# A token tower with a two-expert feed-forward: weight rows stored in pieces, and a first stage with its order and its products rewritten

## What is computed

```python
# token stage (the part that the change touches most)
def vgcn(word_emb, gv_ids, adj, W, b):
    ev = word_emb[gv_ids]                         # 128 table rows for each sequence
    H = jnp.einsum('bgh,bhd->bgd', adj, ev)
    return relu(H.mean(axis=1) @ W.T + b)         # 16 features for each sequence
emb = word_emb[input_ids] + pos_emb
graph = concat([vgcn(...adj0), vgcn(...adj1), vgcn(...adj2)])   # repeated over the 128 tokens
y = layernorm(concat([emb, graph]) @ W_proj.T + b_proj)
# second stage: y + long convolution of layernorm(y) along the batch-major sequence of tokens
h = y + fft_conv(layernorm(y), k) + bias * layernorm(y)
# third stage: 8 experts, 2 for each token
logits = layernorm(h) @ Wr.T;  top-2, softmax over the two
out = h + sum_k w_k * (gelu(x @ Wi[e_k].T + bi[e_k]) @ Wo[e_k].T + bo[e_k])
```

## Time and profile before

| what | us |
|---|---|
| median of 3 runs | 1231.76 |
| the profiled execution's own time | 1239.12 |
| its span in the profile | 1237.3 |
| TensorE busy | 878.2 |
| VectorE busy | 639.1 |
| ScalarE busy | 540.3 |
| GpSimd busy | 674.0 |

### The profile page before, as it was taken

How to read it: one execution, slowest core, us unless ns; L and a number is a source line. 1 busy time by engine, 2 the same in 40 slices (tenths; PEclk the granted TensorE clock), 3 DMA queues, 4 the chain that set the end, 5 groups by cost and what they waited for, 6 DMA issues and landing times. The chain is left out here.

```text
span 1237.3 us, 22985 instructions
## 1 busy us (share of the span) xinstructions
PE 878.2 (71%) x7442; PEld 775.1 (63%) x7442; DVE 639.1 (52%) x2223; ACT 540.3 (44%) x1323; POOL 674.0 (54%) x608
## 2 busy tenths in 40 slices
PE   1544444654444547495875799998988998999991
PEld 0433333443333435495874689998988998998991
DVE  2043434453534354537868745664655565655661
ACT  1021212121212123354855757665655766676760
POOL 6455554655554650002530057776866887878874
PEclk9966666666666667696556989998999999999996
DMA  6234343543535351591088054477477446434442
GB/s 202 74 106 143 108 143 116 147 156 96 163 87 168 95 178 36 144 285 55 1 233 270 3 169 80 59 169 178 57 176 213 62 94 162 62 56 62 62 52 30
DMA packets 119542, 146.94 MB, mean 119 GB/s; under 512 B 13476, under 2 KB 105799, under 8 KB 117415
## 3 DMA queue, kind: packets, MB, share of 16 engines
q0 software_dynamic: 39552, 53.26, 23.1%
q1 hardware_dynamic: 78902, 82.31, 21.8%
q10 hardware_dynamic: 1008, 10.34, 2.1%
HBM read 107.05 MB, written 38.82 MB: 118 GB/s over the span
## 5 line engine op out<-in xcount | busy, mean ns | idle before, releaser
L880 ACT ACTIVATE Hs<-bank,U 128x256 bf16<-128x256 f32 x426 | 211.9, 497 | 183.7 <-PE bank L708 154.0
L517 POOL DMA_INDIRECT out<-Hs,si x142 | 236.9, 1669 | 85.5 <-issue 85.2
L1202 DVE TENSOR_TENSOR Hs<-Hs 128x512 bf16<-128x512 f32 x213 | 147.5, 692 | 148.2 <-ACT Hs L881 134.5
L575 PE MATMUL bank<-ev_g,diag 128*12 128x192 f32 x384 | 96.1, 429 | 179.8 <-ACT diag L759 172.1
L478 POOL DMA_INDIRECT ev_g<-in_word_emb,idx x192 | 185.0, 964 | 58.5 <-issue 58.5
L508 POOL DMA_INDIRECT blob<-xtab_d,gi x142 | 149.0, 1049 | 123.5 <-DVE gi L1187 84.2
L881 ACT ACTIVATE Hs<-bank,U 128x256 f32<-128x256 f32 x426 | 214.0, 502 | 0.0
L723 PE MATMUL bank<-U,Hs 128*128 128x192 bf16 x852 | 213.0, 250 | 0.2 <-issue 0.2
L725 PE MATMUL bank<-U,Hs 128*128 128x192 bf16 x852 | 211.4, 248 | 0.0
L724 PE MATMUL bank<-U,Hs 128*128 128x192 bf16 x852 | 211.1, 248 | 0.0
L575 PEld LDWEIGHTS bank<-ev_g,diag 128*12 128x12 f32 x384 | 44.0, 118 | 231.7 <-issue 119.5
(11 more groups left out here) (184 smaller groups left out, 1726.5 us busy)
## 6 DMA issues: line engine op xcount, KB each, us to landing
U<-blob_d SPq DMA_DIRECT2D x20, 771.0 KB
U<-blob_d SPq DMA_DIRECT2D x20, 672.0 KB
adj_s<-in_adj SPq DMA_DIRECT2D x48, 256.0 KB
ev_g<-kpad_d SPq DMA_DIRECT2D x24, 512.0 KB, 6.2
wst<-in_wsrc SPq DMA_DIRECT2D x8, 1344.0 KB
blob_d<-blob ACTq DMA_DIRECT2D x7, 1443.0 KB
xtab_d<-U SPq DMA_DIRECT2D x4, 1552.0 KB, 8.9
out<-Hs SPq DMA_DIRECT2D x4, 1536.0 KB, 10.9
```

The lines of the kernel that those rows point to most:

```text
L517: pool.indirect_dma_start(out, bass.IndirectOffsetOnAxis(ap=si[:, q % RX, h:h + 1], axis=0), yo[:, q % RX, h, :], None, compute_op=ALU.add ...
L575: last = mm(bank[3][0:KG, 0:D], diag[:, p, k, :], ev_g[:, p, j, b, :], start=k == 0, stop=k == KG - 1)
L880: f(hh[w][:, d, :], ps, ACT.Gelu, bias=bi[:, d:d + 1])
L1202: last = v.tensor_tensor(hl[w][:, c:c + 2, :], hf[w][:, c:c + 2, :], hh[w][:, c:c + 2, :], ALU.subtract)
```

## The change

Two things are in the diff. The prepared weights go to DRAM as `up_d` and `down_d`, each in 6 pieces, so that a run for one partition is 1028 or 896 bytes. And the first stage is rewritten: the index copy goes, and gathers take their indices straight from `ids_i`, in an unrolled loop; the embedding gathers wait on `emb_t` of the quad two before, and only those for `ev_g` on `gvec`; `adj_s` is loaded with four consecutive rows of a matrix in one partition (2048 bytes in one run) and the column means add up over four products with a block-wise `mean_w`; TensorE does the column means of quad i + 1 ahead of the graph vectors of quad i; the graph vectors are computed transposed, with `ev_g` as the weights and one column of means as the moving side, so that `diag`, `grow_s` and the transposes of the result go; `wg` is padded with zeros to 128 columns.

```diff
-        blob_d = nc.dram_tensor("blob_d", (E, 128, BLOB), fp32).ap()
+        up_d = nc.dram_tensor("up_d", (E, PIECES, 128, UP // PIECES), fp32).ap()
+        down_d = nc.dram_tensor("down_d", (E, PIECES, 128, DOWN // PIECES), fp32).ap()
+
+        def pieces(room):
+            return room.rearrange("p (n x) -> p n x", n=PIECES)
+
+        def of_expert(pieces_d, e):
+            return pieces_d[bass.ds(e, 1), :, :, :].rearrange("e n p x -> p (e n) x")
...
         def store_expert(eng, e):
             eng.wait_ge(w_lo, e + 1)
-            eng.dma_start(blob_d[bass.ds(e, 1), :, :].rearrange("e p x -> p (e x)"), blob[:, :]).then_inc(w_out, 16)
+            eng.dma_start(of_expert(up_d, e), pieces(blob[:, 0:UP])).then_inc(w_out, 16)
+            eng.dma_start(of_expert(down_d, e), pieces(blob[:, UP:BLOB])).then_inc(w_out, 16)
...
             def load_adj(i, p):
                 for j in range(GRAPHS):
-                    sp.dma_start(adj_s[:, p, j, :, :],
-                                 t["adj"][j][bass.ds(i * Q, Q), :, :].rearrange("b g h -> g b h")).then_inc(adj_in[p], 16)
+                    sp.dma_start(adj_s[:, p, j, :, :].rearrange("p r h -> p (r h)"),
+                                 t["adj"][j][bass.ds(i * Q, Q), :, :].rearrange("b (c r) h -> (b c) (r h)", r=Q)).then_inc(adj_in[p], 16)
...
             def load_up(e, w):
-                sp.dma_start(wbuf[w][:, 0:UP], blob_d[bass.ds(e, 1), :, 0:UP].rearrange("e p x -> p (e x)")).then_inc(wi_in[w], 16)
+                sp.dma_start(pieces(wbuf[w][:, 0:UP]), of_expert(up_d, e)).then_inc(wi_in[w], 16)
...
-            def gathers(i, p):
-
-                if not (isinstance(i, int) and i < 2):
-                    pool.wait_ge(gvec, i - 1)
-                nc.gpsimd.tensor_copy(idx[:, p, :].rearrange("p (j b) -> p j b", b=Q), ids_i[:, :, bass.ds(i * Q, Q)]).then_inc(idx_staged, 1)
-                pool.wait_ge(idx_staged, i + 1)
-                pool.sem_inc(pool_turn, 1)
+            def gathers(i):
+                p = i % 2
+                after(pool, emb_t, i - 1)
                 for b in range(Q):
                     pool.indirect_dma_start(emb_g[:, p, b, :], None, t["word_emb"],
-                                            bass.IndirectOffsetOnAxis(ap=idx[:, p, b:b + 1], axis=0)).then_inc(emb_in[p], 16)
+                                            bass.IndirectOffsetOnAxis(ap=ids_i[:, 0, i * Q + b:i * Q + b + 1], axis=0)).then_inc(emb_in[p], 16)
+                after(pool, gvec, i - 1)
                 for j in range(GRAPHS):
...
-            def quad(it, p):
-                i = 2 * it + p
-                pe.wait_ge(adj_in[p], 16 * GRAPHS * (it + 1))
+            def column_means(n, i, p):
+                pe.wait_ge(adj_in[p], 16 * GRAPHS * n)
+                after(pe, cs_ready, i)
...
+            def graph_vectors(it, i, p):
+                pe.wait_ge(cs_ready, i + 1)
+                after(pe, gfeat_ready, i)
                 pe.wait_ge(ev_in[p], 16 * KG * (it + 1))
...
+                        mm(bank[3][:, k:k + 1], ev_g[:, p, j, b, 0:D0], cs[:, p, k:k + 1], start=True, stop=True)
+                        last = mm(bank[3][:, 16 + k:17 + k], ev_g[:, p, j, b, D - 128:D], cs[:, p, k:k + 1], start=True, stop=True)
...
+                    i = 2 * it + p
+                    turn_embeddings(it, i, p)
+                    if not (isinstance(i, int) and i == NQ - 1):
+                        column_means(it + 1 + p, i + 1, 1 - p)
+                    graph_vectors(it, i, p)
+                    graph_features(i)
+                    project(i, p)
...
             def pairs(it):
...
+                for p in range(2):
+                    i = 2 * it + p
+                    embedding_copy(i, p)
+                    if not (isinstance(i, int) and i == NQ - 1):
+                        column_copy(i + 1, 1 - p)
+                    graphs(i, p)
+                    if p:
+                        split_hi(it)
+                    if not (isinstance(i, int) and i == 0):
+                        normal(i - 1, 1 - p)
```

More of the change, by code:

```diff
@@ L21 @@
 XROW = 2 * D + 4
+PIECES = 6
+assert UP % PIECES == 0 and DOWN % PIECES == 0
 TS = 256
@@ L340, in _ @@
             load(scale_shift[:, :], t["gamma_beta"].partition_broadcast(128))
-            for c, rows in ((0, D0), (1, D1)):
-                own = bass.AP(tensor=wg, offset=c * GRAPHS * GRAPHS * GD,
-                              ap=[[2 * GRAPHS * GRAPHS * GD, rows], [(GRAPHS + 1) * GD, GRAPHS], [1, GD]])
+            pitch = 2 * GRAPHS * 128
+            for c, first, rows in ((0, 0, D0), (1, 128 - D1, D1)):
+                own = bass.AP(tensor=wg, offset=first * pitch + c * GRAPHS * 128 + D1,
+                              ap=[[pitch, rows], [128 + GD, GRAPHS], [1, GD]])
                 load(own, t["WgT"][c * D0:c * D0 + rows, :].rearrange("d (j g) -> d j g", j=GRAPHS))
@@ L552, in _, with turn_embeddings @@
             pe.wait_ge(cast_done, 1)
-            def quad(it, p):
-                i = 2 * it + p
-                pe.wait_ge(adj_in[p], 16 * GRAPHS * (it + 1))
+            def column_means(n, i, p):
+                pe.wait_ge(adj_in[p], 16 * GRAPHS * n)
+                after(pe, cs_ready, i)
                 for j in range(GRAPHS):
-                    for b in range(Q):
-                        k = p * KG + j * Q + b
-                        last = mm(bank[0][:, k:k + 1], adj_s[:, p, j, b, :], mean_w[:, :], start=True, stop=True)
+                    k = p * KG + j * Q
+                    for r in range(Q):
+                        last = mm(bank[0][:, k:k + Q], adj_s[:, p, j, r, :], mean_w[:, :], start=r == 0, stop=r == Q - 1)
                 last.then_inc(colsum, 1)
+            def turn_embeddings(it, i, p):
                 after(pe, xt_ready, i)
@@ L597, in pair @@
                 for p in range(2):
-                    quad(it, p)
-            steps(pe, NQ // 2, pair)
+                    i = 2 * it + p
[5 more added lines that the diff above has]
+                    project(i, p)
+            column_means(1, 0, 0)
+            steps(pe, NQ // 2, pair, last=1)
             pe.wait_ge(rows_done, NQ)
@@ L752, in _, with column_copy, embedding_copy @@
             f(dec[0:D1, 1, :], trow[0:D1, :], ACT.Exp, scale=filt[0:D1, 1, 3:4]).then_inc(dec_done, 1)
-            def quad(it, p):
-                i = 2 * it + p
+            def column_copy(i, p):
                 act.wait_ge(colsum, i + 1)
-                on_diag = bass.AP(tensor=diag, offset=p * KG * KG, ap=[[2 * KG * KG, 128], [KG + 1, KG]])
-                f(on_diag, bank[0][:, p * KG:(p + 1) * KG], ACT.Copy).then_inc(diag_ready, 1)
+                after(act, gvec, i - 1)
+                f(cs[:, p, :], bank[0][:, p * KG:(p + 1) * KG], ACT.Copy).then_inc(cs_ready, 1)
+            def embedding_copy(i, p):
                 act.wait_ge(emb_t, i + 1)
@@ L790, in pairs @@
             def pairs(it):
-                quad(it, 0)
-                graphs(it, 0)
-                if not (isinstance(it, int) and it == 0):
-                    normal(2 * it - 1, 1)
-                quad(it, 1)
-                split_hi(it)
-                graphs(it, 1)
-                normal(2 * it, 0)
+                for p in range(2):
[8 more added lines that the diff above has]
+                        normal(i - 1, 1 - p)
                 if not (isinstance(it, int) and it > 0):
                     store_expert(act, it)
+            column_copy(0, 0)
             steps(act, NQ // 2, pairs, last=1)
@@ L1150, in _ @@
             fence()
-            dve.wait_ge(w_out, 16 * E)
+            dve.wait_ge(w_out, 32 * E)
             def hots(it):
```

67 lines of the change are left out of this document (26 added, 41 removed).

## The result

The changed kernel takes 1220.62 us (median, 1216.83 to 1223.65) where the kernel before takes 1233.24 beside it: ratio 0.99, 95% interval 0.987 to 0.993. That is a gain of 12 us, not 96, and it lies above the predicted range (1088 to 1176). A second comparison, on a chip of the same kind, gave 0.9905 (0.9872 to 0.9938).

A forecast was written before the change was run, and what follows sets the result against it. A ring of waits with held signals bounds the first stage; -90 us there and -6 in the third stage give -96, from 1239.1 to 1143 profiled, 1136 us as median (1231.8 - 96), range 1088 to 1176.

The forecast's parts named there:

- The ring: First stage: ScalarE, TensorE and GpSimd wait on each other in a loop, period 30.25 us a quad, 23.2 after the change.
- held signal: First stage: what TensorE signals late in a burst of gathers arrives when the burst is through; column sums 14 us late.
- rival 3: First stage: no holding, GpSimd alone sets the pace, 1070 us; chance 0.13 with what lies between it and the forecast.
- 24 products of the shape of the column means' 12, so twice 2.95 = 5.9 us: First stage: length claimed for the transposed graph vectors of one quad, 5.9 us.
- 5 us to spare on TensorE: First stage: TensorE's slack in each 23.2 us period after the change, at the full clock.
- rival 2: First stage: a signal held within 3 us of a burst's start, or more weakly the lower clock, slows it: 1340 us; chance 0.05.
- R + 17.5: First stage: TensorE finishes the graph vectors 17.5 us after R, when a burst is through and held signals arrive.
- rival 1: First stage: VectorE becomes the bound, its slow phase beginning earlier; period 26.2 us, total 1172 us; chance 0.20.
- The third stage, -6 us: Third stage: gathered packets behind 1 KB runs are served sooner, cutting TensorE's fetch waits; -6 us, bounds -14.6 to +5.
- The estimate from the Trainium skill: Third stage weight reloads: 5 reads for 1028 bytes where 4 would do, a quarter more engine time, 0 instead of -6.
- clears at nothing: Start: the 8 memsets cost nothing, as TensorE's first signal is held to 48 anyway; uncovered, about 1 us.
- I costed the new gathers at 1 us a quad: First stage: the index copy that goes, 1.0 us for each quad and two of them at the start.

The follow-up runs named there:

- groups a, c and e: Follow-up runs made on chips with holding, where the kernel before takes 1228 to 1239 us; each group ran on one chip beside the kernel before.
- a3: Changed kernel without the evidence gathers of two of the three graphs from the third quad on (8 gathers a quad, not 16): 1141 us, one run.
- a4: Changed kernel without any evidence gather from the third quad on (4 gathers a quad, not 16): 1138 us, one run.
- b and d: Groups of follow-up runs made on two chips without holding, where the kernel before takes 1100 us.
- d3: Changed kernel with the graph vectors in the old form, new order kept, on a chip without holding: 1075.0 us, ratio 0.9766 to the kernel before.
- a1: Changed kernel with the graph vectors in the old form, new order kept, on a chip with holding: 1162.6 us, ratio 0.9369 to the kernel before.
- c4: Changed kernel with the 13 clears of `wg` moved behind the start's other VectorE work: 1218.9 us, ratio 0.9885 to the kernel before.
- e2: Kernel before with the diff's new gathers and nothing else, on a chip with holding: 1145.0 us, ratio 0.9332 to the kernel before.
- d1: The changed kernel itself, run again on a chip without holding: 1115.4 us, ratio 1.0151 to the kernel before.
- e1: Old-form graph vectors in the new order, gathers spaced by a GpSimd clear of 256 columns behind each: 1140.4 us, ratio 0.9289 to the kernel before.
- c3: Old-form graph vectors in the new order, GpSimd waiting for the next column means ahead of the last 4 evidence gathers: 1213.5 us, ratio 0.9889 to the kernel before.
- b1: Kernel before with the weights in pieces and nothing else, on a chip without holding: ratio 1.0009 to the kernel before.
- c2: Kernel before with the weights in pieces and nothing else, on a chip with holding: ratio 1.0008 to the kernel before.

## Why the prediction was wrong

- **The ring and the held signal: right, on this chip.** The holding is in every trace of groups a, c and e that gathers in bursts of 12 or more (in a3 and a4, at the start alone), with the release 2 to 3 us behind the last gather. That no transfer explains it is borne out by b and d: there it is absent, and the kernel before takes 1100 us. "No holding" (rival 3) is thus what those chips do, though the changed kernel takes 1115 us there and not the 1070 of rival 3; the old form in the new order takes 1075. The rule of the Trainium skill (SBUF — State Buffer, section "Who interferes with whom") that TensorE and ScalarE never wait on anyone fits the traces of two of the four chips. On the others TensorE's own products come singly while gathers run, and the measurement decides.
- **The failing step: graph vectors as "24 products of the shape of the column means' 12, so twice 2.95 = 5.9 us", and with it "5 us to spare on TensorE".** The size holds at the full clock alone (5.6 us). In the stage they ran mostly at 0.50: 10.4 us. I had the lower clock as a clause of rival 2 (R + 27) and priced the forecast at the full one, although gave 0.68 on the mean. That put a full-clock price in the place of the old form's 5.95 us of the earlier trace rows, which stood at 0.68, and the swap looked free:

```profile
320.00:326.00 6.00, 5.95 (x24) 2.74 (x24) 4.68 (x18) 3.38 (x4) 0.00 (x0) 0.68 0.44 131
```

  At the full clock the old form takes 4.07 us, the new one 5.6. The old one's row there, of d3:

```profile
52.30:56.40 4.10, 4.06 (x25) 2.14 (x24) 3.23 (x15) 0.19 (x2) 3.19 (x4) 1.00 0.33 85
```

  And I let the burst hold TensorE's signals but not its work: 5.0 us of gaps a quad. From the end of one group to the start of the next it is 12.3 us in the mean (features, projection, transposes and means, with 12 full-width weight loads in the features, 2.72 us for 1.15), and the group takes 15.5: together the measured period of 27.8, where I had R + 17.5 for the chain. TensorE is the bound, GpSimd waits. It took both terms: by an estimate from these numbers 12.3 + 10.4 = 22.7 us without the gaps, and 12.3 + 5.6 + 5.0 = 22.9 at the full clock, would each have stayed under the 23.2 of my ring. a1 takes the form back and gives 24.3 (forecast 23.4) and 1163 us.
- **In the sum.** The convolution starts at 498.1, not at 423.1: 75 us. The first graph vectors end at 69.0, not 57.1: 12, of which 4.5 is the group's length, 2.2 the second quad's means (5.12 us for 2.95) and 4 the first means, seen at 52.05 instead of 48.1. From there to the end of quad 13's graph vectors it is 13 periods of 28.1 us, not 23.4: 61. The last 2 lie in the end of the stage. From the start of the convolution to the end of the span it is 723.4 us, for 723.9 before: 5.5 of the 6 us forecast for the third stage are missing. That is the 81 us between 1143 and the profiled 1223.65.
- **VectorE** was never the bound: rival 1 fell. That it is slowed late in a burst was right.
- **The third stage, -6 us: wrong**, it was the lower bound, 0. The fetches' wait did not move with the size of the run, so a gather behind 1 KB is not seen to be served sooner than one behind 6 KB. The estimate from the Trainium skill (DMA: Bandwidth & Descriptors, section "How a descriptor splits into AXI transactions"), by which the sum would have had 0 there, was right in the sum; its quarter more engine time was 12%.
- **The start** (clears at nothing): wrong by 4 us. The clears and what follows are drawn out 10 us by VectorE's slow phase, which I had not applied to the start, and the first sums come after the burst is through. In c4, with the clears out of the way, they are seen at 48.21, my 48.1.
- **What I missed as a part.** I costed the new gathers at 1 us a quad, for the copy. That they alone bring the period to 23.9, close to the 23.4 I gave the whole change, came out only in e2. The new order shows nothing beyond it (a1 0.9369, e2 0.9332), but these two ran on two chips and were not compared on one. The transposed form takes most of it away (0.9369 to 0.9905 on one chip).

## What to carry to other kernels

When a change swaps one product form for another on an engine off the bound, price both at the same clock, the lower one as well as the full one, and with the widest idle or stalled stretch beside it. Both forms lengthen with a lower clock here (the new one 5.6 us near the full clock and 10.4 at 0.50, the old one 4.07 at 1.00 and 7.0 at a mean of 0.57); what the swap costs is their difference at the clock that the stage gets. Split a change into the parts that can run alone before reading a mechanism into the whole: here one part held the gain, one did nothing and one lost it. And run a kernel whose time rests on an unexplained wait on more than one chip; here the old form in the new order won on both kinds (a1, d3), the changed kernel on one alone.

## What the runs showed of the hardware

- Chips differ by more than the change: 1100 us (b, d) and 1228 to 1239 us (a, c, e) for the same kernel. One chip was used twice (a, c) and was alike both times; the others once. On the slower ones signals wait for the end of a run of gathers, TensorE's products come singly 2.1 us apart, and VectorE's instructions lie 1.4 us apart. VectorE at the start, changed kernel of the first comparison, then d1:

```profile
15.88 0.12 DVE L918 MEMSET wg<- 64x80 f32 x1 [1.14 <-issue]
...
17.29 0.14 DVE L918 MEMSET wg<- 128x96 f32 x1 [1.24 <-issue]
```

```profile
14.70 0.12 DVE L918 MEMSET wg<- 64x80 f32 x1
...
14.93 0.14 DVE L918 MEMSET wg<- 128x96 f32 x1
```

- What causes it stays open. With 8 or 4 gathers a quad there is none of it (a3, a4, behind the start), a pace of 1.44 us (e1) and a pause of 2 us (c3) do not end it, and the share of the DMA engines is low while it lasts (0.24 from 306.4 to 314.3).
- The old form's 12 products with few weight columns take 4.07 us at the full clock and 5.7 at a mean of 0.70 (d3), 7.0 at 0.57 (b1); the 24 transposed ones 5.6 at 0.95 and, at 0.50, 10.4.
- Weight reloads in runs of about 1 KB take 12% more time of the DMA engines than in runs of 5 to 6 KB (17.1% for 15.3% of the 16 engines, c2), and the kernel no more.
